# A graph attention layer: where the per-chunk softmax work stands among the long products, on one Trainium2 core

## The reference, cut to what matters

```python
qkv = (h @ W_qkv + b_qkv).reshape(n, 3, H, DH)        # n = 3125, H = 8 heads, DH = 32
q, k, v = (qkv[:, 0], qkv[:, 1], qkv[:, 2])
score = jnp.einsum('ehd,ehd->eh', q[dst], k[src]) * SCALE
mx = jax.ops.segment_max(score, dst, num_segments=n)
ex = jnp.exp(score - mx[dst])
denom = jax.ops.segment_sum(ex, dst, num_segments=n)
attn = ex / denom[dst]
msg = attn[:, :, None] * v[src]
h_new = jax.ops.segment_sum(msg, dst, num_segments=n)
```

## Time and profile before

| what | value |
|---|---|
| time, median of 3 runs | 2173.61 us (2172.92 to 2175.29) |
| the profiled execution: time / span | 2170.23 us / 2168.5 us |
| PE, DVE, ACT, POOL busy over the span | 82%, 71%, 49%, 53% |
| mean granted TensorE clock over the span | 0.899 |
| this stage, in the span | about 1240 to 1933 us |

### The profile page before, as it was taken

One profiled execution on the slowest core, in us unless ns is written; L12 is line 12 of the kernel. 1 busy time (PEld: TensorE's weight loads), 2 busy tenths in 40 slices (PEclk: granted clock), 3 DMA queues, 4 the chain that ended last, 5 costly groups with the idle time before them and its releaser, 6 DMA issues. The chain is left out here.

```text
span 2168.5 us, 42934 instructions
## 1 busy us (share of the span) xinstructions
PE 1775.5 (82%) x10388; PEld 1548.7 (71%) x10389; DVE 1534.9 (71%) x2788; ACT 1070.4 (49%) x2353; POOL 1146.4 (53%) x1169
## 2 busy tenths in 40 slices
PE   4699999999999989639946778888888888866278
PEld 3499999999999978629935556666666666645267
DVE  5388888888888836525546578888888788847722
ACT  1677777777777736314401254444444454316133
POOL 0376666666666501644425377776667677512112
PEclk7799999999999989769977899999999999978579
DMA  3443333333333212134306476666556666423310
GB/s 100 131 122 106 106 107 108 104 107 106 106 107 104 82 49 76 68 132 121 117 27 207 153 199 190 186 184 174 169 167 176 173 175 176 134 63 127 121 40 31
DMA packets 132542, 267.46 MB, mean 123 GB/s; under 512 B 24030, under 2 KB 75888, under 8 KB 132407
## 3 DMA queue, kind: packets, MB, share of 16 engines
q0 software_dynamic: 63456, 191.61, 30.4%
q1 hardware_dynamic: 68534, 73.21, 11.0%
q10 hardware_dynamic: 416, 1.18, 0.1%
HBM read 225.34 MB, written 42.50 MB: 124 GB/s over the span
## 5 line engine op out<-in xcount | busy, mean ns | idle before, releaser
L318 POOL DMA_INDIRECT e_rows<-h_table,e_idx x440 | 453.7, 1031 | 213.8 <-issue 106.9
L1739 POOL DMA_INDIRECT a_rows<-kv_table,a_idx x440 | 460.9, 1047 | 184.9 <-issue 144.3
L1816 PE MATMUL a_q<-q,a_spread 128*128 x880 | 246.2, 429 | 9.7 <-ACT a_spread L1790 5.9
L618 PE MATMUL e_w<-w2h,e_hidl 128*128 128x256 f32 x880 | 247.7, 304 | 2.9 <-DVE e_msg L703 2.9
L588 PE MATMUL e_agg<-e_msg,e_hot 128*128 128x256 f32 x880 | 246.1, 402 | 0.0
L1840 PE MATMUL a_agg<-a_rows,x 128*128 128x264 f32 x880 | 226.8, 403 | 0.0
L619 PE MATMUL e_w<-w2l,e_hidh 128*128 128x256 f32 x880 | 226.4, 280 | 0.0
L1816 PEld LDWEIGHTS a_q<-q,a_spread 128*128 128x128 f32 x880 | 177.3, 209 | 42.0 <-issue 13.0
L703 DVE TENSOR_TENSOR e_msg<-e_w,e_rows 128x1024 f32<-128x1024 f32 x110 | 134.7, 1225 | 93.4 <-PE e_w L622 91.8
L1758 ACT ACTIVATE a_apart<-iota_n,dst_rel 128x128 f32<-128x128 f32 x440 | 140.8, 392 | 107.3 <-PE a_agg L1840 106.8
L1840 PEld LDWEIGHTS a_agg<-a_rows,x 128*128 128x128 f32 x880 | 169.9, 202 | 25.0
(11 more groups left out here) (454 smaller groups left out, 4218.2 us busy)
## 6 DMA issues: line engine op xcount, KB each, us to landing
e_ea<-in_eaT SPq DMA_DIRECT2D x220, 64.0 KB
m_rows<-expert_rows SPq DMA_DIRECT2D x32, 272.0 KB, 2.8
e_rows<-h_table,e_idx POOLq DMA_INDIRECT x440
a_rows<-kv_table,a_idx POOLq DMA_INDIRECT x440, 3.7
q_ab<-expert_out SPq DMA_DIRECT2D x50, 128.0 KB, 3.3
kv_table<-q_kv SPq DMA_DIRECT2D x25, 256.0 KB, 2.2
u_stage<-in_m_w SPq DMA_DIRECT2D x16, 256.0 KB
x<-in_x SPq DMA_DIRECT2D x1, 3200.0 KB, 13.5
```

What stands on the lines that cost most here:

```text
L318: c.nc.gpsimd.indirect_dma_start(out=rows[:, g.slot8, j, :], out_offset=None, in_=table, in_offset=bass.IndirectOffsetOnAxis(ap=idx[:, g.s ...
L618: mm(w, hidl[:, g.slot, cols[k]], w2h[:, k, :], start=(k == 0), stop=False)
L1739: nc.gpsimd.indirect_dma_start(out=rows[:, g.slot * IG + j, 0:2 * D], out_offset=None, in_=c.kv_dram, in_offset=bass.IndirectOffsetOnAxis( ...
L1816: last = mm(qp[g.pair][:, j * D:(j + 1) * D], spread[:, g.pair, j, :], window(c.q, wins[j // CT]), start=True, stop=True)
```

## The change

The arithmetic stays the same; instructions change places, and three semaphores are added so that a value is waited for at a later point than directly behind the instruction that makes it.

- PE: the transposition of the exponentials (L1849) leaves the end of place 1 and goes to the middle of place 2's query products, behind the first four of the eight matmuls. `grow` (L1853) follows behind the eight.
- ACT: the copy of the exponentials beside the rows (L1777) goes to the head of place 2. `spread` (L1790) goes ahead of the two exponentials.
- DVE: at place 2 the products (L1905) go ahead of the messages (L1891). At place 0 the first scan (`run`) goes ahead of the products, at place 1 the mask (`mine`) does. The copy of the chunk carry (L1934) leaves place 0, where a scan waited for it, for place 3 ahead of the products.

```diff
-    CHAIN = 7
+    CHAIN = 4
...
# ACT
                     i = at(0)
-                    if i.place == 1 and closed(i.chunk - 1):
+                    if i.place == 2 and closed(i.chunk - 1):
                         ch = i.chunk - 1
-                        need(act, s_ag, (s_df, ch + 1), (s_xT, ch))
-                        nc.scalar.activation(exT[:, :], diff[:, :], ACT.Exp, scale=SCALE).then_inc(s_exp, 1)
-                        need(act, s_ag, (s_fl, ch + 1), (s_fi, 2 * ch))
-                        nc.scalar.activation(factor[:, :], fall[:, :], ACT.Exp, scale=SCALE).then_inc(s_f, 1)
                         need(act, s_ag, (s_xT, ch + 1))
...
# PE
                         for j in range(IG):
+                            if j == CT and i.place == 2 and closed(ch):
+                                pe.wait_ge(s_exp, ch + 1)
+                                tr(exs, exT[:, :], c.ident[:, :]).then_inc(s_xT, 1)
                             last = mm(qp[g.pair][:, j * D:(j + 1) * D], spread[:, g.pair, j, :], window(c.q, wins[j // CT]), start=True, stop=True)
                         last.then_inc(s_q, 1)
+                    if i.place == 2 and closed(ch):
...
+                        need(pe, None, (s_fi, 2 * ch + 2), (s_ex, ch + 1), own=True)
+                        mm(grow, first[:, :], diag[:, :], start=True, stop=True).then_inc(s_gr, 1)
...
-                    if i.place == 1 and closed(ch):
-
-                        need(pe, None, (s_exp, ch + 1), own=True)
-                        tr(exs, exT[:, :], c.ident[:, :]).then_inc(s_xT, 1)
-                    if i.place == 1 and closed(ch):
-
-                        need(pe, None, (s_fi, 2 * ch + 2), (s_ex, ch + 1), own=True)
-                        mm(grow, first[:, :], diag[:, :], start=True, stop=True).then_inc(s_gr, 1)
...
# DVE; products, messages and crossing are the old code, each in a function
+                    if i.place == 2:
+                        products(i)
+                    messages(at)
+                    crossing(i, ch)
+                    if i.place == 3 and closed(ch + 1):
+                        v.tensor_copy(c.carried[:, 0, 0:1], c.carried[:, 0, CH:CH + 1]).then_inc(s_kept, 1)
+                    if i.place == 0 and closed(ch):
+                        link = linked(ch, 0)
+
+                        need(dve, s_dg, (s_sT, ch + 1), (s_new, 2 * ch + 2))
+                        v.tensor_tensor_scan(run[:, :], new[:, 0:P], scT, NEG, ALU.add, ALU.max).then_inc(s_run, 1)
+                    if i.place == 1 and closed(ch):
+
+                        need(dve, s_dg, (s_ca, ch + 1))
+                        v.tensor_tensor(mine[:, :, :], carries.rearrange("p (a t) -> p a t", a=2)[:, :, 0:CH], own, ALU.mult).then_inc(s_mine, 1)
+                    if i.place != 2:
+                        products(i)
```

More of the change, by code:

```diff
@@ L1717, in attention_edges @@
         s_idx, s_hot, s_ht, s_sp, s_q, s_pr, s_sc, s_msg, s_agg, s_acc, s_dg, s_ag, s_ap = (c.sem("a_" + n) for n in names)
-        names = ("scT", "chain", "ends", "tails", "scans", "carries", "diff", "fall", "exp", "factor", "first", "grow", "exT", "ex", "rescaled", "next", "new")
-        s_sT, s_v, s_en, s_tl, s_cs, s_ca, s_df, s_fl, s_exp, s_f, s_fi, s_gr, s_xT, s_ex, s_rs, s_next, s_new = (c.sem("a_" + n) for n in names)
+        names = ("scT", "chain", "ends", "tails", "scans", "carries", "diff", "fall", "exp", "factor", "first", "grow", "exT", "ex", "rescaled", "next", "new", "run", "mine", "carriedkept")
+        s_sT, s_v, s_en, s_tl, s_cs, s_ca, s_df, s_fl, s_exp, s_f, s_fi, s_gr, s_xT, s_ex, s_rs, s_next, s_new, s_run, s_mine, s_kept = (c.sem("a_" + n) for n in names)
         four = lambda g: slice(g.slot * IG, (g.slot + 1) * IG)
@@ L1747, in step @@
                 def step(at):
+                    i = at(0)
+                    if i.place == 2 and closed(i.chunk - 1):
+                        ch = i.chunk - 1
+                        need(act, s_ag, (s_xT, ch + 1))
+                        t = 0
+                        while t < CH // IG:
+                            at_slot = at(t - 2 - CH // IG)
+                            k = 1
+                            while t + k < CH // IG and at_slot.slot + k < R:
+                                k += 1
+                            if real(at_slot):
+                                k = min(k, NIG - at_slot.n) if isinstance(at_slot.n, int) else k
+                                last = nc.scalar.copy(rows[:, at_slot.slot * IG:(at_slot.slot + k) * IG, 2 * D:ROW],
+                                                      exs[:, t * IG * H:(t + k) * IG * H].rearrange("p (t h) -> p t h", h=H))
+                            t += k
+                        last.then_inc(s_ex, 1)
                     g = at(4)
@@ L1760, in step @@
                         nc.scalar.activation(hot[:, four(g), :], apart[:, :, :], ACT.Relu, bias=1.0, scale=-1.0).then_inc(s_hot, 1)
-                    i = at(0)
+                    h = at(2)
+                    if real(h):
+                        need(act, s_ag, (s_ht, h.n + 1), (s_q, h.n - 1))
+                        nc.scalar.copy(spread[:, h.pair, :, :].rearrange("p a n -> p (a n)"), hT[:, :]).then_inc(s_sp, 1)
                     if i.place == 1 and closed(i.chunk - 1):
@@ L1767, in step @@
                         nc.scalar.activation(factor[:, :], fall[:, :], ACT.Exp, scale=SCALE).then_inc(s_f, 1)
[L1768 to L1780, removed]
                     if i.place == 2 and closed(i.chunk):
@@ L1785, in step @@
                         nc.scalar.copy(passes[:, :, :], c.passes[:, :, bass.ds(i.chunk, 1), :].rearrange("p w a t -> p w (a t)")).then_inc(s_new, 1)
[L1786 to L1790, removed]
                 rounds(act, step, 4, LAG + 1, Edges)
@@ L1815, in step @@
                         for j in range(IG):
+                            if j == CT and i.place == 2 and closed(ch):
+                                pe.wait_ge(s_exp, ch + 1)
+                                tr(exs, exT[:, :], c.ident[:, :]).then_inc(s_xT, 1)
                             last = mm(qp[g.pair][:, j * D:(j + 1) * D], spread[:, g.pair, j, :], window(c.q, wins[j // CT]), start=True, stop=True)
                         last.then_inc(s_q, 1)
+                    if i.place == 2 and closed(ch):
+                        if not real(g):
+                            pe.wait_ge(s_exp, ch + 1)
+                            tr(exs, exT[:, :], c.ident[:, :]).then_inc(s_xT, 1)
+                        need(pe, None, (s_fi, 2 * ch + 2), (s_ex, ch + 1), own=True)
+                        mm(grow, first[:, :], diag[:, :], start=True, stop=True).then_inc(s_gr, 1)
                     m = at(-LAG)
@@ L1874, in linked, with messages, products, crossing @@
                     return link
+                def messages(at):
+                    m = at(-LAG)
+                    if real(m):
+                        need(dve, s_dg, (s_ex, m.chunk + 1))
+                        ex = rows[:, four(m), 2 * D:ROW].rearrange("p t (h a) -> p t h a", a=1).broadcast_to([P, IG, H, DH])
+                        v.tensor_tensor(by_head(rows[:, four(m), D:2 * D]), by_head(rows[:, four(m), D:2 * D]), ex, ALU.mult).then_inc(s_msg, 1)
+                        ahead.fetch(at(0).then, "sums", m.n)
+                def products(i):
+                    if real(i):
+                        need(dve, s_dg, (s_q, i.n + 1), (s_rows[i.slot], (i.turn + 1) * 64))
+                        keys = rows[:, four(i), 0:D]
+                        v.tensor_tensor(keys, qp[i.pair][:, :].rearrange("p (a d) -> p a d", a=IG), keys, ALU.mult).then_inc(s_pr, 1)
+                def crossing(i, ch):
+                    if i.place == 2 and closed(ch):
+                        w = ahead.take(i.step, "crossing", ch * (CH // IG))
+                        need(dve, s_dg, (s_gr, ch + 1), (s_acc, i.n - LAG))
+                        to = c.agg[:, bass.ds(w, 1), 0:D].rearrange("p a (h d) -> p (a h) d", h=H)
+                        v.scalar_tensor_tensor(to, grow.rearrange("p (h a) -> p h a", a=1).broadcast_to([P, H, DH]), 1.0, to, ALU.add, ALU.mult).then_inc(s_rs, 1)
+                        to = flat(c.agg[:, bass.ds(w, 1), D:DM])
+                        v.scalar_tensor_tensor(to, grow, 1.0, to, ALU.add, ALU.mult).then_inc(s_rs, 1)
                 def step(at):
@@ L1908, in step @@
                     if i.place == 0 and closed(ch):
-                        link = linked(ch, 0)
-                        need(dve, s_dg, (s_sT, ch + 1), (s_new, 2 * ch + 2))
-                        link(v.tensor_tensor_scan(run[:, :], new[:, 0:P], scT, NEG, ALU.add, ALU.max))
+                        need(dve, s_dg, (s_run, ch + 1))
                         link(v.tensor_tensor_scan(back(peak[:, :]), back(new[:, 1:P + 1]), back(run[:, :]), NEG, ALU.add, ALU.max))
@@ L1915, in step @@
                     if i.place == 1 and closed(ch):
-                        link = linked(ch, 3)
```

(8 more changed lines are left out.)

## The result

The changed kernel takes 2150.1 us (median of 4, 2147.3 to 2154.6), the one before 2174.5 (4 runs beside it). The ratio is 0.9886, 95% interval 0.9863 to 0.991: 24 us less. The prediction was 2161, a gain of 12.3; the measured gain is twice that. The profiled execution of the changed kernel took 2147.3 us (span 2145.5), 22.9 less than that of before.

A forecast was written before the change was run, and what follows sets the result against it. A ring of DVE and PE, neither alone, was taken as the bound. Shorter chunks (7.3 us) and the clock (5) sum to 12.3, so 2173.6 - 12.3 = 2161.3, put as 2161; own range 2150 to 2168, overall 2136 to 2177.

The forecast's parts named there:

- The chunk without a spell: One exT to the next with no stretch at 1.2 GHz: 22.12 to 21.85 us, 7.3 us over 27 chunks.
- the number of spells: Stretches at clock 0.50 (1.2 GHz): 18 expected, two thirds of 27 chunks, near the 19 counted before.
- Places 0, 1 and 3: DVE's scan, mask and carry copy moves: places 3 and 0 from 10.32 to 9.85 us, place 1 6.71 to 6.50.
- Place 2: Messages behind the products release PE's aggregation later: 5.50 us against 5.09, the gain given away.
- PE's idle time: Place 2: PE's waits for exT and diag, 1.83 us together, come back as one 1.8 us wait before the aggregation.
- The clock: Cost of spells at 1.2 GHz: 19 x 1.69 = 32 us before, 18 x 1.5 = 27 after, a gain of 5.
- rival C: The spell doubles behind the idle block: in all 18 chunks 15 us more, 2188; chance 0.10.
- the 0.2 us of slack: Slack ahead of PE's next aggregation, taken to cut a spell from 1.67 to 1.5 us.
- Where the spells would begin: Around the place-2 aggregation on PE, no longer in the query products of place 2.
- long and short chunks would alternate: New chunks of 21.85 us without a spell and 23.35 with one would alternate; no row shows how often such are hit.
- POOL: Next floor: 16 gathers take 21.6 us a chunk, just below 21.85; as the bound it gives 2203, chance 0.04.

The follow-up runs named there:

- e1: Kernel before with only the DVE moves of places 0, 1 and 3; PE, ACT and place 2 as before: 2142.2 us, ratio 0.9862.
- e2: Changed kernel with first scan, mask and carry copy back in their old places; PE, ACT and place 2 moves kept: 2169.9 us, ratio 0.9993.
- e3: Changed kernel with messages ahead of the products again at place 2: 2127.6 us, ratio 0.9802.
- e4: Changed kernel with grow behind the transpositions of place 2 and eight added clearing matmuls ahead of PE's wait for the messages: 2133.2 us, ratio 0.983.
- e5: Changed kernel with grow alone moved behind the transpositions of place 2, no added clears: 2151.2 us, ratio 0.9903.
- e6: Changed kernel with two of the four gathers of a group left out from the eleventh group on, output not the reference's: 2150.7 us, ratio 0.9897.
- e9: Changed kernel with messages first at place 2 and PE's register loads ahead of its wait before grow: 2132.0 us, ratio 0.9821.

## Why the prediction was right, and where it was off

The time lies at the lower edge of the forecast's own range, 2150 to 2168, and the gain is twice the one given. The chunk without a spell was right in each of its parts; the number of spells was not.

*Places 0, 1 and 3.* Right. The self-waits that the long products now cover gave 0.75 us a chunk in e1, 0.68 predicted.

*Place 2.* Right, in size too: 5.49 against 5.50. The reason given, that messages behind the products hold back PE's aggregation, is shown by e2 (0.40 longer) and e3 (0.88 shorter). The prediction took this as the price of a trade. The trade did not pay: what it bought, the moves on PE and ACT, is worth 14.6 us (e3 against e1), and it cost 18 to 22 (the changed kernel against e3). The scans alone do at least as well as the whole change (2142 and 2150, intervals 0.9839 to 0.9884 and 0.9863 to 0.991, which overlap). Nor was it needed, for with the messages first the exponentials still come in time (e3).

*PE's idle time.* 1.8 us in front of the aggregation was predicted and is there, as 1.12 + 0.65. But the prediction had one block released by the messages. It missed the register loads, which stand behind `grow`'s wait in PE's program and start only once that is over. They cost nothing here, since PE would have waited for the messages anyway.

*The clock.* This is the term that was mis-sized. It said 19 x 1.69 = 32 us today and 18 x 1.5 = 27 then, a gain of 5; it was 23 spells and 14, at 1.69 and 1.68, a gain of 15. Three errors: it counted chunks with a spell and not spells, so the five chunks with two (the clock column shows 0.86 to 0.88; rival C speaks of two such) counted once; two thirds of the chunks was a guess where half are hit; and the 0.2 us of slack that should cheapen a spell did not show. Where the spells would begin it had right: all 14 begin at the clearing matmul or in the aggregation of place 2. The one of the chunk at 1504.06 stretches the aggregation from 1.95 to 3.63 us:

```profile
1508.64 3.63 PE L1852 MATMUL a_agg<-a_rows,x 128*128 128x264 f32 x8
```

That the changed kernel's spells follow from PE's idle block is shown by e4 against e5. Three of the nine that are gone had another place. In the kernel before, each of the three chunks with a loop turn has its second spell at place 1, behind PE's waits for DVE's masked ends and carried scan. One of them in the timeline, and behind it the clock, in the columns of the earlier trace rows:

```profile
1604.31 0.23 PE L1845 MATMUL a_misc<-a_ends,rows_of_head 128*8 128x32 f32 x2 [1.11 <-DVE a_ends L1914]
1606.00 0.41 PE L1808 MATMUL a_misc<-carried,heads_of_row 8*128 8x34 f32 x2 [1.46 <-DVE carried L1936]
...
1606.50:1610.00 3.50, 3.50 (x10) 0.51 0.67 186
```

The same two waits in a chunk with a turn after the change, where no spell follows:

```profile
1591.43 0.23 PE L1857 MATMUL a_misc<-a_ends,rows_of_head 128*8 128x32 f32 x2 [0.17 <-DVE a_ends L1942]
1592.83 0.41 PE L1810 MATMUL a_misc<-carried,heads_of_row 8*128 8x34 f32 x2 [1.17 <-DVE carried L1961]
```

With the DVE moves (e1 and the changed kernel) none of the three such chunks has a spell there; without them (before and e2) three and two of three have. So by these four traces the DVE moves, counted in the prediction for the length of the chunk alone, also took away these three. Why the other six are gone is open. The prediction's remark that long and short chunks would alternate holds in e1 (11 of 14), at a chunk of 21.4, but not in the changed kernel, where 8 of 13 chunks with a spell are followed by another; so the length of the chunk by itself does not explain it. Spell counts of one profile also move by one or two (14, 16 and 14 in three kernels with the same chunk).

*POOL.* It does not bound the changed kernel, as e6 shows; the one before was not tried, but there POOL waits 36.1 us for free slots. The room is small: a gather in the changed kernel takes longer. No more of them meet the messages (157 of 385, 169 of 378 before), but those that do take 1.38 us on the mean and not 1.18; all others take 0.95 in both kernels. The groups of 1290 to 1840 us, against the earlier trace rows:

```profile
L1739 POOL DMA_INDIRECT a_rows<-kv_table,a_idx x385 | 433.2, 1125 | 118.1 <-issue 104.4 <-PE a_agg L1852 7.3 <-ACT a_idx L1768 6.4
```

433.2 + 118.1 is the whole stretch, and 118.1 is 0.31 for each of 385: POOL hardly pauses. At 1.125 + 0.31 us a gather it needs 23.0 us for the 16 of a chunk, and a chunk lasts 23.2 on the mean of all 26, so it just keeps pace. In e3 it is what sets the pace: 386 gathers fill 540 us there, also with 0.30 between them, which is 22.4 us for 16, and the chunks last 22.4 on the mean of the 26.

## What to carry to other kernels

Where two engines form a ring, count each step as the chain through both, and put the instruction that the other engine waits for first; moving independent work in front of it costs most of its length (0.88 us here for a product of 1.14), while moving short self-waiting instructions around a long one only gains. Split a change that has two parts, and test each with and without the other: here one part was worth 14.6 us and another cost more than that. Count the spells of a lowered clock one by one from the clock column of short stretches, price them apart from the waits, and try cheap matmuls in the idle block: they gave 12 to 17 us here. After each gain ask what engine has no pause left.

## What the runs showed of the hardware that was not expected

A wait in front of PE's register loads brings them into view: two loads kept PE idle for 1.12 us ahead of the next matmul (29.9 us in all in e3), and 13.2 us in all (3.2 there and 10.0 ahead of `grow`) when they stood ahead of that wait in e9.

Some 1.2 us of matmuls on zeros in an idle block of 1.8 us kept the granted clock at 1.00 in all but one of 26 chunks (e4); without them 14 and 16 had a spell.

A gather that starts just ahead of the messages can lose more than their whole length. In the changed kernel's timeline:

```profile
1530.46 2.26 POOL L1739 DMA_INDIRECT a_rows<-kv_table,a_idx  x1 [0.30 <-issue]
...
1530.70 1.20 DVE L1887 TENSOR_TENSOR a_rows<-a_rows 128x1024 f32<-128x1024 f32 x1
```

It takes 2.26 us instead of 0.95 and ends 0.82 us after the messages, as the one in the earlier trace rows did; so does one gather for nearly every one of the messages (92 of 95 here, 93 of 93 before), and no gather that misses the messages takes more than 0.97. The mean gather went from 1.050 to 1.125 us although its own work did not change.
